# The second attention in 64-row strips with split operands, paired banks, and its maxima placed by VectorE

## What is computed

```python
nx = _layernorm(x, ln1_w, ln1_b)
qkv = nx @ Wqkv + bqkv
q, k, v = jnp.split(qkv, 3, axis=-1)
q = q.reshape(B, S, N_HEADS, HEAD_DIM)
...
scores = jnp.einsum('bqhd,bkhd->bhqk', q, k) / jnp.sqrt(jnp.float32(HEAD_DIM))
causal = jnp.tril(jnp.ones((S, S), bool))
scores = jnp.where(causal, scores, jnp.finfo(scores.dtype).min)
attn = jax.nn.softmax(scores, axis=-1)
out = jnp.einsum('bhqk,bkhd->bqhd', attn, v).reshape(B, S, D)
return out @ Wo + bo
```

## Time and profile before

| | |
|---|---|
| Median of 3 runs | 1764.53 us (1761.92 to 1767.25) |
| Profiled execution, its own time | 1764.11 us |
| Its span | 1762.3 us |
| TensorE busy | 1617.1 us, 92% of the span |
| VectorE busy | 1156.6 us, 66% |
| ScalarE busy | 913.4 us, 52% |
| GpSimd busy | 352.4 us, 20% |
| Second attention, from 364.7 to 629.9 us | 265.2 us |

### The profile page before, as it was taken

How to read it: one execution, slowest core, us unless ns; L and a number is a source line. 1 busy time by engine, 2 the same in 40 slices (tenths; PEclk the granted TensorE clock), 3 DMA queues, 4 the chain that set the end, 5 groups by cost and what they waited for, 6 DMA issues and landing times.

```text
span 1762.3 us, 33014 instructions
## 1 busy us (share of the span) xinstructions
PE 1617.1 (92%) x11293; PEld 1090.1 (62%) x11294; DVE 1156.6 (66%) x3098; ACT 913.4 (52%) x2098; POOL 352.4 (20%) x405
## 2 busy tenths in 40 slices
PE   8998989988888786999999799999999999989998
PEld 6555555543333364999997344566666666667887
DVE  4776666755555448554444788876776776767776
ACT  2887878635555552444444466756755765620000
POOL 1111111102442121111111420352322322110000
PEclk9999999889999996999999899999999999999999
DMA  8787778400000054566565311100100010020001
GB/s 300 257 287 255 268 252 283 165 6 1 1 1 2 1 189 138 204 203 202 192 201 170 96 42 37 55 13 25 31 25 28 16 31 13 13 84 1 1 0 48
DMA packets 82883, 182.16 MB, mean 103 GB/s; under 512 B 7521, under 2 KB 50145, under 8 KB 78273
## 3 DMA queue, kind: packets, MB, share of 16 engines
q1 hardware_dynamic: 79344, 171.15, 28.9%
q0 software_dynamic: 3408, 9.31, 1.9%
HBM read 129.19 MB, written 51.25 MB: 102 GB/s over the span
## 4 chain that ended last, share of the span: by engine, by line
PE 78%; DVE 10%; ACT 8%; issue 3%; DMA 0%; POOL 0%; DVEq 0%; SPq 0%; ACTq 0%; POOLq 0%
PE PS L1428 9%; PE PS L1264 8%; PE PS L835 7%; PE PS L1383 6%; PE PS L1299 5%; PE PS L1398 5%; PE PS L1373 5%; PE PS L1055 5%; PE PS L902 4%; PE PS L1247 4%; PE PS L924 4%; PE PS L1354 3%; PE PS L935 2%; PE PS L1075 2%; PE PS L1249 2%
## 5 line engine op out<-in xcount | busy, mean ns | idle before, releaser
L1864 ACT ACTIVATE P<-PS,nm 128x512 f32<-128x512 f32 x256 | 174.6, 695 | 108.2 <-DVE nm L2472 92.2
L1383 PEld LDWEIGHTS PS<-idf,P 128*128 128x128 f32 x1024 | 118.1, 143 | 98.4 <-issue 64.2
L2151 DVE CUSTOM_DVE_ANT_0 dump<-PS,maskw 128x256 f32<-128x256 f32 (+3 forms) x256 | 114.8, 488 | 92.1 <-PE PS L1060 86.9
L2063 DVE CUSTOM_DVE_ANT_0 SN<-PS,SR 128x128 f32<-128x128 f32 (+3 forms) x256 | 115.3, 488 | 87.8 <-PE PS L906 87.7
L1383 PE MATMUL PS<-idf,P 128*128 128x128 f32 x1024 | 155.8, 282 | 12.0 <-ACT PTb L1874 10.5
L2472 DVE TENSOR_REDUCE nm<-PS 128x2 f32<-128x1024 f32 x128 | 150.5, 1216 | 23.9 <-PE PS L1373 23.8
L1264 PE MATMUL PS<-xT,W1c 128*128 128x128 f32 x1248 | 145.9, 275 | 1.8 <-ACT xT L1789 1.8
L1264 PEld LDWEIGHTS PS<-xT,W1c 128*128 128x128 f32 x1248 | 142.6, 192 | 4.0 <-ACT xT L1789 2.3
L1055 PE MATMUL PS<-QP,KP 32*128 32x128 f32 (+3 forms) x512 | 107.7, 493 | 36.7 <-ACT PTf L1720 33.5
L1720 ACT ACTIVATE PTf<-PS 128x512 f32<-128x512 f32 (+3 forms) x256 | 98.0, 435 | 82.8 <-PE PS L1055 82.7
L1599 ACT ACTIVATE SN<-SN,nm 128x128 f32<-128x128 f32 (+3 forms) x256 | 128.8, 556 | 7.0 <-DVE nm L2063 6.9
(11 more groups left out here) (352 smaller groups left out, 3494.2 us busy)
## 6 DMA issues: line engine op xcount, KB each, us to landing
W1c<-in_fc1T SPq DMA_DIRECT2D x39, 1024.0 KB, 5.4
SR<-rel SPq DMA_DIRECT2D x16, 1024.0 KB, 7.5
rel<-EN SPq DMA_DIRECT2D x15, 1024.0 KB, 4.8
SR<-rel SPq DMA_DIRECT2D x16, 768.0 KB, 6.7
rel<-EN SPq DMA_DIRECT2D x15, 768.0 KB, 4.3
SR<-rel SPq DMA_DIRECT2D x16, 512.0 KB, 4.6
W2f<-in_fc2T SPq DMA_DIRECT2D x8, 1024.0 KB, 7.6
rel<-EN SPq DMA_DIRECT2D x15, 512.0 KB, 3.2
```

The costliest lines, as they stand in the source:

```text
L1383: last = nc.tensor.transpose(TR1[j][:, c * P:c * P + P], P1[s % 4][:, j, c * P:c * P + P], idf[:])
L1864: last = af(P1[s % 4][:, j, :], PD[s % 2][:, j, :], ACT.Exp, bias=nm1[:, s % 4, j:j + 1], accum_out=sm1[:, s % 4, j:j + 1])
```

## The change

Each step's operands become 64-row strips of fp32r. Projected keys and queries are kept once as a rounded part (written by ScalarE) and a remainder (written by VectorE) in `HK` and `HQs`. For every job, twelve transfers on SyncE's queue copy 16-row pieces of them into `KD` and `QD`, so that one product of 48 rows holds rounded x rounded, rounded x remainder and remainder x rounded. GpSimd fills these tiles' constant rows once, at the end of the first attention.

The maxima are taken by one reduction over a pair of banks (`NB`, a single pair). The causal mask is added by two bf16 products into the same banks. After a job's last reduction VectorE places the maxima's rounded part and remainder into `MX`; TensorE turns them as before, ScalarE copies them to `MS`, and a second product per strip, `MS` by the same keys, subtracts them. The transposed scores use two bank pairs and one exponential of double width per step. The side products get two banks in turn (`MBF`), are cut in parts spread over the steps, and the value products are spread over steps 2 to 4. The first four projections and the first three row steps move into the end of the first attention. `W2_ORDER` and two loads' semaphores follow from the new layout; they add no transfer.

```diff
-Q_STEP, P_STEP, OT_STEP, MX_STEP = 0, 2, 4, 6
+V_STEPS = {2: (0,), 3: (1, 2), 4: (3,)}
+MX_STEP, OT_STEP = 6, 7
+HS, DQ, DM = P // 2, 3 * DH0, 4
+NKD, NQD = 5, 4
+FIRST_H = [(NJ - 2, 2), (NJ - 2, 5), (NJ - 1, 1), (NJ - 1, 4)]
+FIRST_G = 5
...
-        STB, MB = PS[4:7], PS[7]
+        MB = PS[7]
+        NB, STB, MBF = PD[0], PD[1:3], PS[6:8]
...
+            def strips(kind, m, to, halves, parts):
+                b, g = divmod(m, HGS)
+                for x in range(2):
+                    rows = slice(DH0 * (HQ * x + g), DH0 * (HQ * x + g) + DH0)
+                    for i, part in enumerate(parts):
+                        o = HS * x + DH0 * i
+                        sp.dma_start(to[o:o + DH0].bitcast(F32), halves[rows, part].bitcast(F32))\
+                            .then_inc(strip_sem[kind][m % RING[kind]], 16)
...
+                    if s >= 2:
+                        pe.wait_ge(f_ex, s - 1)
+                    bank = lambda x: STB[s % 2][:, x, 0:S - c * P]
+                    keys = lambda x: KD[n % NKD][HS * x:HS * x + HS, t, c * P:c * P + P]
+                    for x in range(2):
+                        mm(bank(x), keys(x), QD[n % NQD][HS * x:HS * x + HS, t, c * P:S], start=True, stop=False)
+                    for x in range(2):
+                        last = mm(bank(x), keys(x), MS[n % 2][HS * x:HS * x + HS, c * P:S], start=False, stop=True)
+                    last.then_inc(f_st, 1)
+                if m < NJ:
+                    if i == 0:
+                        strips_loaded(pe, "k", m)
+                        strips_loaded(pe, "q", m)
+                    if g >= 1:
+                        pe.wait_ge(f_max, g)
+                    for x in range(2):
+                        mm(NB[:, x, 0:w], QD[m % NQD][HS * x:HS * x + HS, y, r * P:r * P + P],
+                           KD[m % NKD][HS * x:HS * x + HS, y, 0:w], start=True, stop=False, skip_group_check=True)
+                    for x in range(2):
+                        last = mm(NB[:, x, w - P:w], idh[:], maskh[:], start=False, stop=True, skip_group_check=True)
+                    last.then_inc(f_nat, 1)
...
+            def high_h(bank, kind, half):
+                to, c = (HK, COLS["bqkv"] + 2 + half) if kind == "hk" else (HQs, COLS["bqkv"] + half)
+                af(to[:, 0, half], bank[:], ACT.Identity, bias=cols[:, c:c + 1]).then_inc(f_hi, 1)
...
+                af(PTf[n % 2][c][:, 2 * t:2 * t + 2, :], STB[s % 2][:, :, 0:S - c * P], ACT.Exp, scale=DH0 ** -0.5)\
+                    .then_inc(f_ex, 1)
...
+            def row_max(g):
+                m, i = divmod(g, NUF)
+                r, y = F_ROWS[i], 1 - i % 2
+                w = P * r + P
+                dve.wait_ge(f_nat, g + 1)
+                last = v.tensor_reduce(mxs[m % 2][:, r, :, y], NB[:, :, 0:w], AX.X, ALU.max)
+                last.then_inc(f_max, 1)
+                if i == NUF - 1:
...
+                    link(v.tensor_copy(at(MX[:].bitcast(F32R), 0), mxs[m % 2][:]))
+                    v.tensor_tensor(at(MX[:], 1), mxs[m % 2][:], at(MX[:], 0), ALU.subtract).then_inc(f_mx, 1)
```

More of the change, by code:

```diff
@@ new lines, in eight_heads_h, with first_heads_h @@
+            def eight_heads_h(bank, kind, b, half, parts=range(DK)):
+                w = WFs[:, :, D:] if kind == "hk" else WFs
+                for k in parts:
+                    last = mm(bank, eight_heads(w, k, half), NT[:, k, b * S:b * S + S], start=(k == 0), stop=(k == DK - 1))
+                return last
+            def first_heads_h(i):
+                if i == 0:
+                    pe.wait_ge(ld["wf"], 16)
+                    pe.wait_ge(a_mr, A_AT["h", 1] + 1)
+                    pe.wait_ge(a_en, 2 * RT + (NJ - 2) * NUA)
+                if i >= 2:
+                    pe.wait_ge(f_hr, i - 1)
+                eight_heads_h(PS[i % 2], "hk" if i < 2 else "hq", 0, i % 2).then_inc(f_hw, 1)
@@ new lines, in values_f @@
+            def values_f(n, cs):
+                if cs[0] == 0:
+                    m_bank(("p", n))
+                bank = MBF[M_AT["p", n] % 2]
+                b, hg = divmod(n, HGS)
+                if hg == 0 and cs[0] == 0:
+                    m_done(pe, ("hv", b, 0))
+                    m_done(pe, ("hv", b, 1))
+                for c in cs:
+                    pe.wait_ge(f_ca, n * RT + c + 1)
+                    for j in range(HQ):
+                        last = mm(bank[HQ8 * j:HQ8 * j + VW0, c * P:S], VE[:, b * RT + c, head_f(hg, j), :],
+                                  PTf[n % 2][c][:, j, :], start=(c == 0), stop=(c == RT - 1), skip_group_check=True)
+                if cs[-1] == RT - 1:
+                    last.then_inc(f_pv, 1)
@@ new lines, in other_f @@
+            def other_f(use, part):
+                if part == 0 or use[0] == "h":
+                    m_bank(use)
+                bank = MBF[M_AT[use] % 2]
+                if use[0] in ("hk", "hq"):
+                    last = eight_heads_h(bank, *use, parts=[part])
+                elif use[0] == "h":
+                    last = tokens_h(bank, use[1])
+                else:
+                    _, b, x = use
+                    tb = b * RT + 2 * x + part
+                    last = project(bank[:, part * D:part * D + D], lambda k: NT[:, k, tb * P:tb * P + P], lambda k: WFv[:, k, :], D)
+                if part == 1:
+                    last.then_inc(m_wrote(use), 1)
@@ new lines, in max_to_rows, with out_to_tokens @@
+            def max_to_rows(n):
+                bank = m_bank(("mx", n))
+                pe.wait_ge(f_mx, n + 1)
+                for r in range(RT):
+                    last = nc.tensor.transpose(bank[:, r * P:r * P + P], MX[:, r, :], idf[:])
+                last.then_inc(m_wrote(("mx", n)), 1)
+            def out_to_tokens(n):
+                m_done(pe, ("p", n))
+                bank = m_bank(("ot", n))
+                for r in range(RT):
+                    last = nc.tensor.transpose(bank[:, r * P:r * P + P], OS[n % 2][:, r * P:r * P + P], idf[:])
+                last.then_inc(m_wrote(("ot", n)), 1)
@@ L2180, in _ @@
+            for g in range(NUF - FIRST_G, AHEAD):
                 row_max(g)
-                if g == NUF + 1:
-                    queries_with_max(0)
             for n in range(NJ + 1):
```

501 lines of the change are left out of this document (246 added, 255 removed).

## The result

The changed kernel took 1750.88 us (median of 12 runs, 1740.19 to 1757.89 but for one disturbed run at 1880.99, its granted clock 0.825 where the others had 0.97), the kernel before 1764.65 (12 runs, 1761.92 to 1767.25): a ratio of 0.9914, 95% interval [0.9897, 0.9932]. Timed again beside the experiments it was 1746.84 against 1769.13, 0.9875 [0.9853, 0.9898]. So it is faster, by 0.9 to 1.2%, where 2.1% was forecast: the direction held, the size didn't. The profiled run took 1747.4 us, 19.2 more than the forecast of 1728.2.

The account below looks back on a forecast made before the run. It took the kernel to be bound by a TensorE-ScalarE-TensorE chain of waits with side-bank copies; the scores' stretch saving 34.5 us and the start 1.4, in all 35.9, gave 1728 us, range 1708 to 1752.

Parts of the forecast that it names:

- The start: Before the transposed scores: they begin near 378.8 us, 1.4 sooner than before, within 4 us sooner or later.
- Below nothing it could go only if the added projections fell on a full TensorE: First attention's end: the 1.4 us gained at the start turns into a loss only if TensorE has no room there.
- The stretch: The 16 jobs of transposed scores, first start to last end: 211.5 us summed, against 246.0 before.
- the 6 reserved for the half clock: Transposed-score stage: 6 us kept for TensorE at half clock, expected before job 0 and at the end.
- products of the scores and rows, 6.2 summed: TensorE's scores, subtraction, rows and masks in one job: 1.03, 0.86, 0.69 and 0.51 us a step by width, 6.2 in all.
- one load of 0.11 for either half of the step: Each step on TensorE: only one uncovered weight load of 0.11 us for the scores' half and one for the rows' half.
- values, 2.28: Value products in steps 2 to 4 of a job: 2.28 us of TensorE, divided among the steps by columns.
- turns, 1.18: Steps 6 and 7 of a job: a turn of 0.59 us each beside the step's own products.
- 0.3 of overhang: VectorE's outputs, remainders and placing in a job: nearly all hidden in its waits for rows, 0.3 us sticking out.
- Rival (3): Light jobs: half clock holds jobs 12, 13 and a third of the others to twice TensorE's time; 10 us, 1738; 8%.
- (2): Side banks: pairing doesn't free TensorE, jobs with projections stay at 15.2 us; 22 us lost, 1750; chance 8%.
- Rival (1): Weight loads of subtraction and masks stay uncovered, 0.11 us more for each; 17 us over 14.5 jobs, 1745; chance 15%.

Follow-up runs that it names:

- e2: The changed kernel without the two mask products of each row step: 1729.48 us, ratio 0.9788 to the kernel before.
- e8: The changed kernel with the values' products one step earlier and spread over steps 1 to 3, without idle products: 1758.8 us in one run.
- e9: The changed kernel with early weight loads, no mask products, and idle products only in the row steps before job 0: 1715.63 us, ratio 0.9705 to the kernel before.
- e10: The changed kernel with early weight loads and no mask products, without any idle products: 1722.59 us, ratio 0.9739 to the kernel before.
- e4: The changed kernel with the rows' maxima 13 steps ahead of the transposed scores instead of 12: 1749.00 us, ratio 0.9900 to the kernel before.
- e6_warm: The changed kernel with idle products in the last eight row steps before job 0 and the first two steps of jobs 12 to 14: 1747.44 us, ratio 0.9869.
- e7_combined: The changed kernel with early weight loads, no mask products, and idle products before job 0 and in most jobs' light steps: 1722.87 us, ratio 0.9748.

## Why the prediction was wrong in size

**The start, 5.8 missing.** The step that failed is "Below nothing it could go only if the added projections fell on a full TensorE". I asked whether TensorE had room and not whether their weights were there. The issue of WFs had stood behind a pass of SyncE's transfers that waits for the first attention's progress; the change moved the projections ahead of it. That is 5.1 us of wait and a projection at half clock behind it, 6.6 to 7.2 us together; from the product ahead of the wait to the scores are 68.3 us for 61.7 before, and 61.5 without the wait. By the forecast they had to be 60.4, so 7.9 are missing on this way, not 5.8: the profiled execution had reached it 2.1 us sooner than the one before the change, which is chance. The row steps were 15.1 from the first wide one on for 14.5, as summed.

**The stretch, 9.2 missing.** Job by job: jobs 1, 4, 5, 8 and 9 were 0.88 longer than the 13.8 summed (4.4 in all), jobs 2 and 3 0.84 (1.7), jobs 6, 7, 10 and 11 0.51 (2.0), 12 and 13 0.61 (1.2), job 0 3.45, job 14 3.8; job 15 was 1.4 shorter, and the 6 reserved for the half clock lie inside jobs 0 and 14. 4.4 + 1.7 + 2.0 + 1.2 + 3.45 + 3.8 - 1.4 - 6 is 9.2.

The terms that were too small, from a job with four half projections, where TensorE is the bound and nothing else can hide:
- products of the scores and rows, 6.2 summed: 6.70. The wide steps were right (1.01 and 1.03); those of 384 took 1.06 and 0.94 for 0.86, of 256 0.77 and 0.68 for 0.69, of 128 0.61 for 0.51. The step that failed is "one load of 0.11 for either half of the step": each change between 64-row and 128-row products shows about 0.1 (0.33 for 0.23), the values start 0.21 behind a mask where a projection starts 0.12 behind it, though all three have 128 rows, and a pair of 128 columns doesn't start within 0.06 of the other but in 0.11;
- values, 2.28: 0.99 + 1.20 + 0.34 = 2.53; I had cut by columns what has a share per product;
- projections, 3.88: 4.07; turns, 1.18: 1.10; and a wait of 0.29 ahead of the second turn.

Together 14.69, where 13.5 and 0.3 of overhang were summed. In jobs 12 and 13 the turns are 1.93, 2.03, 2.03, 2.03, 1.28, 1.39, 1.19 and 1.44, 13.32 where 12.4 and 0.3 were summed; the largest misses are the last (0.34, the wide scores in it) and the first with values (0.26, where TensorE's own work takes 2.03 for 1.77). By its own terms the sum should also have had 1.30 and 0.98 for the two small turns and not 1.28 and 0.96, which is 0.04 a job in the steps where they decide. The jobs differ by what they carry, and every one is the sum over steps of the larger of turn and work; that rule of the prediction held (job lengths repeat to 0.03 us, and the values moved early gave 12.88), its inputs were each a little low and all in one direction. My 0.3 for all overhang was the only reserve against that.

**The half clock.** 6 us were reserved, for job 0 and the end, and that is where it fell: job 0 lost 2.0 to 2.3 (18.0 and 18.3 against 16.0 warmed) and job 14 2.9 in one profile and none in the other, 5.2 us in the first profile and 2.0 in the second. In job 0 the rest is work, 16.0 us and not 14.8, most of it in its last step: a whole projection behind a reduction waited for took 3.41 us there, where 0.51 and 1.95 were to be added. Rival (3), the half clock in light jobs, did not come in the changed kernel. It came in e2, e8, e9 and e10, which made those jobs lighter or shortened their turns and left them without idle products, but also in job 13 of e4, which was no lighter.

**The range.** That 1750.9 lies inside 1708 to 1752 is luck. The forecast's own range, 1712 to 1744, missed it; the stated one reached further for rivals (1) to (3), and (2) and (3) did not come at all.

**What held.** TensorE's waits in the stage (385 to 605 us; total, times, longest), as the earlier trace rows for before:

```profile
PEld PS L1109 <- ACT PTf L1829: 31.9, 55, 1.1
...
PEld PS L1120 <- DVE mxs L2231: 16.7, 44, 1.1
...
PE PS L1120 <- DVE mxs L2231: 8.0, 15, 0.8
```

The products themselves now wait for the reduction, 8.0 us, and once for an exponential, 0.7. The weight loads still stand behind exponentials for 31.9 us in all, under other products for the most part, where 43.0 us stood in 130 us before; that this wait would be nearly gone is true of the products and not of the loads. The turn at 512 columns took 1.93 to 2.03 for 1.93, pairs stand 0.23 apart, placing and VectorE's other work are hidden (VectorE waited 79.1 us for rows), and TensorE waited for no strip behind the start. Rival (1), uncovered loads, is half right: the rows' pair, on the same strips as the subtraction's pair before it and with other weights, starts 0.23 behind it at 512 columns and 0.11 at 256 (516.00 and 511.50 above), so its load is covered; beside 128-row products 0.10 more is seen. The Trainium skill, page "TensorE: Matmul & The Clock Gate", section "Part 3: Packing small matmuls — row/col tiling", says in one sentence that loads overlap running matmuls only where the row group differs, and in another allows it for a background weight buffer too; these rows go against the first and not against the second.

**Open.** The 3.4 us behind the stage. Between the 13 profiles of these kernels that part, on which none of the edits bears, ran from 1137.9 to 1146.6 us, counted from the last scores' start. The one profile of the kernel before has 1136.4, below them all, but a spread of 8.7 leaves open whether the change has any effect there; no run was made to tell.

## What to carry to other kernels

When work is moved to an earlier place, follow its operands as well: a 5 us wait for weights cost 6.6 to 7.2 us with the slow projection behind it, and with the weights in time the moved projections had made the way to the scores no longer (61.5 us, 61.7 before). When a change takes the waits away, the sum has to be made of TensorE's issue distances in the new order, shape change by shape change, since an error of 0.05 us a step is no longer hidden. And a lighter job is not always a shorter one: before shortening TensorE's work beside a chain on VectorE, look at the granted clock in the lightest job, and put idle products only where the trace shows the wait, no longer than it.

## What the runs showed of the hardware

The granted clock fell to its lower level in some executions of the same instructions and not in others (job 14: 14.30 and 11.37 us). An idle fp32 product of 128x128 takes 0.27 to 0.29 us of TensorE's time (in e6_warm five of them, ten records, in 1.33 us; in e7_combined three hold the next product back by 0.86). And 64-row pairs of fp32r cost 0.33 instead of 0.23 at 512 columns when they follow a 128-row product. Behind the same wait of 5 us and with the same instructions the granted clock was 0.50 from 324 to 340 us in e6_warm, and 0.88 and then 1.00 over the same stretch in the changed kernel.
